# Layer 2 of a four-layer graph network: a node tile's steps add up in PSUM slots that ScalarE copies out, and the node's own product is made in layer 2's node stage

## The reference

```
def _L2_gnn_ref(x, edge_src, edge_dst, adj_vals, w_nbr, w_own, bias):
    h = x @ w_nbr
    msgs = adj_vals[:, None] * h[edge_src]
    agg = jax.ops.segment_sum(msgs, edge_dst, num_segments=x.shape[0])
    return agg + x @ w_own + bias

h = jnp.maximum(_layernorm(x, axis=-1), 0.0)
x = x + _L2_gnn_ref(h, src, dst, edge_weight, L2_gnn_w_nbr, L2_gnn_w_own, L2_gnn_bias)
```

## Time and profile before

| | us |
|---|---|
| median of 3 runs | 6134.13 |
| lowest and highest | 6128.75, 6135.93 |
| span of the profiled execution | 7291.3 |
| edge stage 1 in it | 1650 |
| node stage 2 in it | 129 |
| edge stage 2 in it | 1267 |
| node stage 3 in it | 183 |
| edge stage 3 in it | 1774 |

### The profile page before, as it was taken

One profiled execution on the slowest core, in us unless ns is written; L12 is line 12 of the kernel. 1 busy time (PEld: TensorE's weight loads), 2 busy tenths in 40 slices (PEclk: granted clock), 3 DMA queues, 4 the chain that ended last, 5 costly groups with the idle time before them and its releaser, 6 DMA issues. The chain is left out here.

```text
span 7291.3 us, 78521 instructions
## 1 busy us (share of the span) xinstructions
PE 5030.7 (69%) x19221; PEld 3431.7 (47%) x19221; DVE 4716.5 (65%) x11148; ACT 2046.9 (28%) x5654; POOL 3612.8 (50%) x4189
## 2 busy tenths in 40 slices
PE   3799999999467676667655555557466666666687
PEld 2544444447355555555433333334355455545466
DVE  6699999997355555556644444447366666656776
ACT  3688888886110000000200000001111111111143
POOL 4455555552555555544566666652445454544000
PEclk9899999999666666667777777779576766766798
DMA  5533333333332333222233333332222222222201
GB/s 163 198 98 97 98 98 97 97 96 114 97 81 80 82 82 84 79 76 65 85 92 93 92 92 92 92 118 62 72 77 79 76 79 76 80 72 77 73 24 36
DMA packets 410176, 641.70 MB, mean 88 GB/s; under 512 B 182156, under 2 KB 280032, under 8 KB 409334
## 3 DMA queue, kind: packets, MB, share of 16 engines
q0 software_dynamic: 171200, 474.81, 23.3%
q1 hardware_dynamic: 225664, 149.06, 7.0%
q10 hardware_dynamic: 12896, 13.11, 0.5%
HBM read 563.02 MB, written 69.86 MB: 87 GB/s over the span
## 5 line engine op out<-in xcount | busy, mean ns | idle before, releaser
L250 POOL DMA_INDIRECT G<-table,srcI x1760 | 1667.6, 948 | 1649.2 <-PE pM L502 996.0
L502 PE MATMUL pM<-G,one 128*128 128x260 f32 (+1 forms) x3520 | 1414.9, 509 | 258.6 <-DVE G L373 167.5
L384 DVE TENSOR_TENSOR acc<-acc,pM 128x260 f32 (+1 forms) x1760 | 755.3, 429 | 913.6 <-PE pM L502 570.8
L1357 POOL DMA_INDIRECT G<-table,srcI x880 | 830.5, 944 | 611.7 <-ACT zt L1381 497.5
L572 POOL DMA_INDIRECT G<-table,srcI x880 | 832.9, 947 | 434.4 <-issue 192.8
L608 PE MATMUL pM<-G,one 128*128 128x256 f32 x1760 | 647.4, 508 | 576.2 <-DVE one L581 430.4
L1493 PE MATMUL pM<-zt,one 128*128 128x512 f32 x1760 | 950.2, 621 | 122.1 <-DVE acc L1454 45.4
L502 PEld LDWEIGHTS pM<-G,one 128*128 128x128 f32 x3520 | 757.4, 257 | 437.6 <-DVE G L373 212.6
L1381 ACT ACTIVATE zt<-G,a4S 128x128 f32<-128x128 f32 x2640 | 856.1, 389 | 0.0
L428 ACT ACTIVATE oneT<-pT 128x512 f32<-128x512 f32 x440 | 259.6, 597 | 1966.5 <-PE pT L485 866.8
L608 PEld LDWEIGHTS pM<-G,one 128*128 128x128 f32 x1760 | 382.6, 244 | 836.1 <-DVE one L581 561.1
(11 more groups left out here) (316 smaller groups left out, 6598.2 us busy)
## 6 DMA issues: line engine op xcount, KB each, us to landing
G<-table,srcI POOLq DMA_INDIRECT x3520
a10T<-step_a SPq DMA_DIRECT2D x660, 30.0 KB
far<-step_rec SPq DMA_DIRECT2D x224, 64.0 KB
table<-row SPq DMA_DIRECT2D x100, 128.0 KB
acc<-zero SPq DMA_DIRECT2D x21, 512.0 KB
step_a<-part SPq DMA_DIRECT2D x7, 960.0 KB
table<-row SPq DMA_DIRECT2D x50, 132.0 KB
table<-row SPq DMA_DIRECT2D x50, 130.0 KB
```

The source lines that it names most:

```text
L250: pool.indirect_dma_start(G[:, par * C + j, 0:ROW], None, tab, bass.IndirectOffsetOnAxis(ap=srcI[:, k:k + 1], axis=0)).then_inc(s_g[par * ...
L384: nc.vector.tensor_tensor(to, to, pM[j % R][:, :], ALU.add).then_inc(s_acc, 1)
L502: nc.tensor.matmul(pM[j % R][:, :], one[:, par * C + j, :], G[:, par * C + j, :], start=True, stop=True).then_inc(s_m, 1)
L1357: pool.indirect_dma_start(G[:, k % GS, :], None, table[0], bass.IndirectOffsetOnAxis(ap=srcI[:, k:k + 1], axis=0)).then_inc(s_g[k % GS], 16)
```

## The change

In the edge stage of layer 2, PE no longer writes each step into a tile of its own. PSUM holds 8 slots of one bank each (`pS`); all steps of node tile n add into slot n modulo 8 (`start=False`). At each step three more things happen, at slots read from a list (`node_s`, loaded into `slots`): ACT copies the slot of the node tile before this step's into `sums` (`sums[:, n+1, :]` ends as the sum of tile n; it is copied some 17 times, the last copy is the complete one), DVE clears the slot three tiles ahead by copying zeros (`COMING = 3`), and `mark` goes on, with 8 buffers `one` in place of 4. DVE adds the bias to one tile of x in every 17 steps. The own product moves to node stage 2, as a second product of 256 columns per tile (`pO[1]`), which DVE adds to x in place of the bias; `hT` is gone. In node stage 3 POOL adds `sums` to x (`Layer2End.second`) before the statistics of each tile, and SP saves x to `x3` in five parts, each of ten tiles. Setup makes the three rows of the slot list: four small DVE operations and three small scattered DMAs, and one load (`nodeR`) less.

```diff
-                R = 4
-                one = [se.sb(f"one{j}", [P, P]) for j in range(R)]
-                pM = [se.ps(f"pM{j}", [P, D]) for j in range(R)]
+                RO, EVERY, LATE = 8, K // NT, 3
+                one = [se.sb(f"one{j}", [P, P]) for j in range(RO)]
+                slots = se.sb("slots", [1, 3, KP], I32)
...
-                        def add(k, j):
-                            dve.wait_ge(s_m, k + 1)
-                            freed(dve, s_acc, added(k) - 1)
-                            at = tile(acc, node(k, j))
-                            nc.vector.tensor_tensor(at, at, pM[j % R][:, :], ALU.add).then_inc(s_acc, 1)
...
+                        def mark(k):
+                            freed(dve, s_m, k - RO + 1)
...
+                        def clear(k):
+                            if k % 16 == 0:
+                                at.update(listed(dve, slots[0:1, 2, :], k, SLOTS - 1))
+                            freed(dve, s_out, k - COMING)
+                            dve.wait_ge(s_zero, k + 1)
+                            nc.vector.tensor_copy(sum_of(at[k]), nought[:, :]).then_inc(s_zero, 1)
...
+                    @block.scalar
+                    def _(act):
...
+                            if k % 16 == 0:
+                                at.update(listed(act, slots[0:1, 0, :], k, SLOTS - 1))
+                                to.update(listed(act, nodeA[0:1, :], k, NT - 1))
+                            freed(act, s_m, k)
+                            freed(act, s_out, k)
+                            nc.scalar.activation(tile(sums, to[k]), sum_of(at[k]), ACT.Copy).then_inc(s_out, 1)
...
+                            pe.wait_ge(s_zero, max(1, k - COMING + 2))
+                            pe.wait_ge(s_one, k + 1)
+                            pe.wait_ge(s_g[k % u], k // u * 16 + 16)
+                            nc.tensor.matmul(sum_of(at[k]), one[k % RO][:, :], G[k % u][:, :], start=False, stop=True,
+                                             skip_group_check=True).then_inc(s_m, 1)
...
             def dve_end(dve, n, j, pO, row, aux, s_ae, b):
-                return nc.vector.tensor_tensor(tile(x_sb, n), tile(x_sb, n), b[1][:, :], ALU.add)
+                return nc.vector.tensor_tensor(tile(x_sb, n), tile(x_sb, n), pO[1][:, :], ALU.add)
...
+                def stores(self, sp, n):
+
+                    if n % (NT // 5) == 1:
+                        some = slice(n - 1, n - 1 + NT // 5)
+                        sp.wait_ge(self.s_plus, n - 1 + NT // 5)
+                        sp.dma_start(x3.rearrange("(t p) c -> p t c", p=P)[:, some, :], x_sb[:, some, :]).then_inc(self.s_x3, 16)
...
+                def second(self, pool, n):
+                    pool.tensor_tensor(x_sb[:, n, :], x_sb[:, n, :], self.sums[:, n + 1, :], ALU.add).then_inc(self.s_plus, 1)
```

More of the change, by code:

```diff
@@ L34 @@
 H1, H3 = 4, 8
+SLOTS, COMING = 8, 3
 def build(nc, a, out):
@@ L576, in _ @@
                     def _(dve):
[L577 to L581, removed]
-                                                    ALU.is_equal, ALU.mult).then_inc(s_one, 1)
-                        def add(k, j):
-                            dve.wait_ge(s_m, k + 1)
-                            freed(dve, s_acc, added(k) - 1)
[L587 to L591, removed]
-                                dve.wait_ge(s_acc, added(k))
-                                nc.vector.tensor_tensor(acc[:, n, :], acc[:, n, :], pO[n % 2][:, :], ALU.add).then_inc(s_acc, 1)
@@ L594, in _ @@
-                        steps(dve, u, (AHEAD, load), (0, mark), (LAG, add))
-                    @block.sync
-                    def _(sp):
-                        sp.dma_start(w_sb[:, :, :], w_own.rearrange("(c p) n -> p c n", p=P)).then_inc(s_w, 16)
+                        nc.vector.memset(nought[:, :], 0.0)
+                        nc.vector.memset(pS[:, :, 0:D], 0.0).then_inc(s_zero, 1)
+                        at = {}
+                        dve.wait_ge(s_list, 16)
+                        def mark(k):
+                            freed(dve, s_m, k - RO + 1)
+                            nc.vector.tensor_scalar(one[k % RO][:, :], iota[:, :], relS[:, k:k + 1], wS[:, k:k + 1],
+                                                    ALU.is_equal, ALU.mult).then_inc(s_one, 1)
@@ L600, in _ @@
                     @block.tensor
                     def _(pe):
-                        pe.wait_ge(s_w, 16)
-                        def scatter(k, j):
-                            pe.wait_ge(s_one, k + 1)
-                            gathered(pe, u, s_g, k, j)
-                            freed(pe, s_acc, added(k - R))
-                            nc.tensor.matmul(pM[j % R][:, :], one[j % R][:, :], G[j][:, :], start=True, stop=True).then_inc(s_m, 1)
-                            n = own_at(k)
-                            if n is not None:
-                                freed(pe, s_acc, added(EVERY * (n - 1) - 1) + 1 if n >= 2 else 0)
-                                for c in range(2):
-                                    ins = nc.tensor.matmul(pO[n % 2][:, :], hT[:, n, c * P:(c + 1) * P], w_sb[:, c, :], start=(c == 0), stop=(c == 1))
-                                ins.then_inc(s_o, 1)
@@ L958, in _ @@
                                 sp.dma_start(node_f.rearrange("(b p) -> p b", p=P), nkc[:, :]).then_inc(s_ndd, 16)
+                                for q in range(3):
+                                    sp.dma_start(node_s[q, :].rearrange("(b p) -> p b", p=P), slot[:, q, :]).then_inc(s_ndd, 16)
                             sp.wait_ge(s_w1, 128)
@@ L1037, in _ @@
                             link(nc.vector.tensor_scalar(base[:, :], nk[:, :], float(-P), None, ALU.mult))
+                            for q, ahead in enumerate((SLOTS - 1, 0, COMING)):
+                                link(nc.vector.tensor_scalar(slot[:, q, :], nkc[:, :], float(ahead), None, ALU.add))
+                            link(nc.vector.tensor_scalar(slot[:, :, :], slot[:, :, :], SLOTS - 1, None, ALU.bitwise_and))
                             nc.vector.tensor_copy(nki[:, :], nkc[:, :]).then_inc(s_nd, 1)
```

120 lines of the change are left out of this document (74 added, 46 removed).

## The result

The changed kernel takes 6153.48 us (median of 8 runs, 6148.62 to 6157.1), the kernel before 6133.26 in the same series: ratio 1.0033, 95% interval [1.0023, 1.0043]. It is 20 us slower. The forecast was 6159, its own range 6147 to 6185.

What follows compares the result with a forecast made beforehand. Edge stage 2 was taken to be bound by POOL's gathers, near 1100 us in a timed run. Edge stage 2 0, node stage 2 +18, node stage 3 +5, setup +2: 6134 + 25 = 6159 us, likeliest 6147 to 6185, whole 6060 to 6215.

Steps and rivals of the forecast that it cites:

- Edge stage 2, 0 us: Edge stage 2: added operations stay under POOL's 1.25 us per gather, so no change; bounds -170 and +150 us.
- most of PE's holes belong to the profiled execution: Edge stages 1 to 3: PE's late spells mostly absent from timed runs, leaving at most 234 us over the floor.
- the first rival: Edge stages: PE's holes are real and deeper rings close them, half to all of 170 us; 5990 to 6075, chance 0.22.
- Node stage 2, +18 us: Node stage 2: the second product adds 11 us over 9 rounds and 7 us in the last eight tiles.
- two turns (4.6) still fit into 5.9, three turns take 6.9. So a round goes from 11.3 to 12.6 at most: +1.3, of which I take 1.2: Node stage 2, five-tile rounds: PE at 2.3 us a tile lengthens each round, 11 us over 9 rounds.
- The +7 for the last eight tiles: Node stage 2, last eight tiles without `scales`: their ends go from 1.3 to 2.2 us apart, +7 us.
- The second rival: Node stage 2: the second product is hidden; total 6122 to 6146 us, no change, chance 0.2.
- The other end, +50 at the low clock: Node stage 2: at the low clock the product costs 1.7 us more a tile, the stage +50 us.
- Node stage 3, +5 us: Node stage 3: DVE contends with POOL's additions, 10 rounds x 0.5 us = 5 us, from 0 to 10.
- +0.6: Start of node stage 3: additions, `scales` and a statistics precede DVE's first copy, 12.4 us against 11.8, about +0.6.
- Setup, +2 us: Setup: four DVE operations and 2688 four-byte elements during DVE's 24.4 us wait, +2 us; below 1, above 5.
- Behind the last gather, 0 us: After edge stage 3's last gather to the end: no change forecast, 0 us.

Runs made afterwards that it cites:

- e5: The changed kernel with its slot list made by four DVE operations in edge stage 2, without scattered DMAs, second chip: 7321.87 us against 7306.35, ratio 1.0023.
- e1: The kernel before, unchanged, profiled again on a chip where it takes what the timed runs took: span 6123.1 us.
- e6: The changed kernel with both products in node stage 2, but DVE adding the bias from SBUF instead of the own product from PSUM: 7341.01 us against 7306.35, ratio 1.0056.
- e3: The changed kernel without the own product in node stage 2, DVE adding the bias from SBUF as before: 6152.03 us, ratio to the kernel before 1.0035.
- e8: The changed kernel without POOL's 50 additions in node stage 3 and the waits for them: 7329.82 us against 7306.35, ratio 1.0040.
- e4: The kernel before with the slot list's four DVE operations and three scattered DMAs added to setup, unused: 6146.79 us against 6133.85, ratio 1.0024.
- e9: The changed kernel with its slot list made by DVE in edge stage 2, without scattered DMAs, third chip: 6141.55 us against 6135.25, ratio 1.0012.
- e10: The kernel before with the bias added in edge stage 2 and one scattered list less in setup: 6122.95 us against 6135.25, ratio 0.9983.
- e2: The changed kernel with the slot list's three scattered DMAs moved behind the load of x: 6147.35 us, ratio to the kernel before 1.0026.

## Why the prediction was right, and where it was not

**Edge stage 2, 0 us: right, with one reason wrong.** POOL's gather row is untouched (833.5 and 833.3 us busy, 947 ns each), and the stage stays 1110. The operations added came out as estimated: the copy of zeros 429 ns (taken: 0.42), ACT's copy 383, as in the earlier trace rows, and PE is busy for 955 / 880 = 1.09 us a step at a granted clock of 0.58 (taken: 0.92 to 1.1). One thing had no price: `mark` went from 352 to 431 ns, and DVE is busy for 0.84 us a step, not 0.63; why wasn't tried, and under 1.25 it costs nothing. A stretch of the changed kernel's timeline in this stage:

```profile
3399.51 0.95 POOL L551 DMA_INDIRECT G<-table,srcI  x1 [0.30 <-issue]
...
3400.76 0.95 POOL L551 DMA_INDIRECT G<-table,srcI  x1 [0.30 <-issue]
...
3401.28 0.38 ACT L602 ACTIVATE sums<-pS  x1 [0.81 <-PE pS L616]
...
3401.80 0.43 DVE L577 COPY pS<-nought 128x256 f32 x1 [0.29 <-ACT sums L602]
3402.01 0.95 POOL L551 DMA_INDIRECT G<-table,srcI  x1 [0.30 <-issue]
```

The gathers follow each other at 1.25 us without a wait, and in that time the other engines, which wait for each other in turn, do their step. The prediction's estimate of 0.33 us for a copy with an SBUF source was too low here. It comes from a row of the Trainium skill, "VectorE: DVE Perf Modes", section on the TRN2 errata, and the same section says that this row under-predicts the time of a single operation; the 429 ns agree with that. What was wrong is "most of PE's holes belong to the profiled execution". They go with the chip: the kernel before takes 7284 to 7329 us in all 28 timed runs on the second chip, and the profiles taken there have the holes. The first profile's chip isn't on record, but its 7291 us lie in that range. The conclusion held because the runs that were forecast came from a chip without the holes, which the prediction couldn't know: that part is luck. And the first rival fails where the holes are real too: with eight `one` buffers and slots, e5's edge stage 2 took 1272.4 us on the second chip, against 1266.0 for the kernel before in the first profile.

**Node stage 2, +18 us: wrong, +0.8.** The step that failed is "two turns (4.6) still fit into 5.9, three turns take 6.9. So a round goes from 11.3 to 12.6 at most: +1.3, of which I take 1.2". POOL's row that begins a round, in e1:

```profile
3028.27 0.20 POOL L764 TENSOR_TENSOR mean<-bn 128x5 f32<-128x5 f32 x1 [2.48 <-DVE bn L817]
...
3039.55 0.20 POOL L764 TENSOR_TENSOR mean<-bn 128x5 f32<-128x5 f32 x1 [2.49 <-DVE bn L817]
```

and in the changed kernel, with ACT's copies out of PSUM between:

```profile
3045.79 0.20 POOL L764 TENSOR_TENSOR mean<-bn 128x5 f32<-128x5 f32 x1 [2.06 <-DVE bn L815]
...
3046.02 0.38 ACT L1680 ACTIVATE row<-pO 128x256 f32<-128x256 f32 x1 [1.07 <-PE pO L859]
...
3047.96 0.38 ACT L1680 ACTIVATE row<-pO 128x256 f32<-128x256 f32 x1 [1.08 <-PE pO L859]
...
3050.91 3.65 POOL L1674 TENSOR_TENSOR acc<-acc,xr 128x256 f32<-128x256 f32 x5
...
3056.62 0.20 POOL L764 TENSOR_TENSOR mean<-bn 128x5 f32<-128x5 f32 x1 [2.06 <-DVE bn L815]
```

A round went from 11.28 down to 10.83. Two terms were off. A turn that PE bounds takes 1.94 us (3046.02 to 3047.96), not 2.3: PE runs at the full clock there (granted 1.00 over this round, 0.80 in e1's), and the 1.4 I started from held more than PE's own work, for at the full clock two transposes follow each other in e1 after 1.12 us (3029.84, 3030.96). Five turns of 1.94 are 9.7 us and fit into a round of 11.3: in e6, with both products and the old operand, the round stays at 11.30. (The prediction's own figures, 5.9 + 6.9, would have been 12.8, not 12.6.) And I costed DVE's end at nothing, as an addition for an addition. Its operand moved from SBUF to PSUM, and beside POOL's additions that is 0.41 us in place of 0.94, on the mean of the stage 411 ns in place of 498; the earlier trace rows had shown the effect on L1667, and I used it for node stage 3 only. e3 and e6 split it: the product +5.7 us, the operand -4.8. The +7 for the last eight tiles held nearly: from the end of the last `scales` to the last copy it is 9.2 us in e1 and 15.0 in the changed kernel, +5.8. The second rival ("the second product is hidden") was right for the rounds and for the sum of the stage, but not for its end, and it gave the total wrongly. The other end, +50 at the low clock, didn't come: the stage's granted clock rose to 0.92.

**Node stage 3, +5 us: measured +1.3.** The 5 us were for DVE beside POOL's additions. From PE's first product to the end of the stage it takes 170.8 us in e1 and 172.9 in the changed kernel, and 170.4 in e8 against 173.6 in e5: 2.1 and 3.2 us, so the mechanism is there and the size was high. The start, which I had put at "+0.6", came out as a gain of 0.9 us: the additions cost 3.3 there (e8), and without the one save of x beside the weights' loads the start gains more than that.

**Setup, +2 us: wrong, and the size that mattered.** "2688 four-byte elements that go out while DVE waits 24.4 us for gathered rows; below 1, above 5". The wait was read as cover. It is a wait for DMAs, and more DMAs lengthen it. Windows of four microseconds of the setup, e1 and then the changed kernel, each with its DMA queues from 44 to 48 us (q0 has the gathers):

```profile
44.00:48.00 4.00, 0.00 (x0) 0.00 (x0) 0.00 (x0) 0.00 (x0) 2.92 (x4) 1.00 1.10 73
48.00:52.00 4.00, 0.00 (x0) 0.00 (x0) 1.01 (x2) 0.00 (x0) 3.09 (x4) 1.00 0.62 143
...
q1 hardware_dynamic: 335, 0.21, 79.4%
q0 software_dynamic: 38, 0.09, 31.0%
```

```profile
44.00:48.00 4.00, 0.00 (x0) 0.00 (x0) 0.00 (x0) 0.00 (x0) 2.98 (x4) 1.00 1.93 1
48.00:52.00 4.00, 0.00 (x0) 0.00 (x0) 0.00 (x0) 0.00 (x0) 2.89 (x4) 1.00 1.48 21
...
DMA packets 1196, 0.00 MB, mean 1 GB/s; under 512 B 1196, under 2 KB 1196, under 8 KB 1196
q1 hardware_dynamic: 1196, 0.00, 193.4%
```

In the changed kernel the DMA engines move 1 GB/s from 44 to 48 us, in 1196 small packets (the share adds up the packets' times, which overlap, and so goes to 1.93), and no packet of the gathers' queue begins in that time: the gathers of the destinations stand still beside the elements. The Trainium skill, "DMA: Bandwidth & Descriptors", says in the table of its section "Specifications" that a transfer below 512 bytes is a read-modify-write, and in the table of "Rules for kernel authors" that a last dimension that isn't contiguous becomes one descriptor per element. By that these 10.5 KB are 2688 small writes; the trace agrees with 2800 more packets under 512 B on the page. That each is a read-modify-write no run here shows. The slot list's DMAs with their DVE operations cost 12.9 us (e4), and with the DMAs gone 14 of the 20 us go (from 1.0033 to 1.0012): by the medians the term is 13 to 14 us, by the profiles 18.7.

**Behind the last gather, 0 us: +3.9, not foreseen.** The code is the same in both. Two parts can be told apart. One goes with the program: from the issue of the last store to the end it takes 10.0 to 10.1 us in all seven profiles with the old edge stage 2 and 11.5 to 11.7 in all seven with the new one, whatever the chip. The other is a pattern in the two batch norms. ACT's squares (a ring of four with DVE's and PE's parts) wait for DVE 9 times in the changed kernel and 10 in e9, 4 times in e1 and e10, and from its first to its last square each norm takes some 1.2 us longer (23.7 and 23.3 us against 22.3 and 22.2); 1.0 of that comes back between the two. This pattern doesn't follow the program: e2, with the new edge stage 2, has the short norms (4 waits, 512.8 us behind the last gather), and the first profile, with the old one, the long ones (8 waits, 23.6 and 23.3 us). Why the same instructions fall into another pattern, and what the 1.6 us are, wasn't tried.

So the total was right by luck, by two errors of opposite sign: 17 us too much in node stage 2, and in the setup 17 too little by the profiles, 11 to 12 by the medians.

## What to carry over

A wait for DMAs covers work on engines, not further DMAs: before small transfers are put into such a wait, ask which transfers share the DMA engines with them, and count their elements, for bytes didn't set the price here. An operation that is exchanged for one of the same shape isn't free of price when its operand moves between SBUF and PSUM and another engine works beside it; and where POOL and DVE set a stage's round, a second product per tile costs nothing in the rounds and shows only in the tiles behind them (5.7 us here), while one DVE addition per tile less gives 13 us, of which 5 went back where the addition was put (e10). A rewritten inner loop gains nothing while the gathers ahead of it keep their 1.25 us.

## What the runs showed of the hardware that was not expected

The same kernel takes 6134 us on two of the chips and 7306 and 7444 on two others, steadily. The difference lies in three stages: by the profiles of the kernel before, edge stage 1 takes 1650 against 1167 us, edge stage 2 1266 against 1110, and edge stage 3 to the end 2212 against 1702, while the setup (133, 131), edge stage 0 (1438, 1423) and node stages 2 and 3 (129.7 and 128.9, 183.9 and 183.7) agree within 2%. In the first profile's edge stage 2 PE stands still for 3.46 and for 6.94 us before two rows, and DVE around them:

```profile
4200.84 0.42 DVE L588 TENSOR_TENSOR acc<-acc,pM 128x256 f32 x1 [3.48 <-DMA xr<-x]
4201.58 0.70 PE L608 MATMUL pM<-G,one 128*128 128x256 f32 x2 [3.46 <-DVE one L581]
4205.06 0.42 DVE L588 TENSOR_TENSOR acc<-acc,pM 128x256 f32 x1 [3.53 <-DMA xr<-x]
4208.48 0.42 DVE L593 TENSOR_TENSOR acc<-acc,pO 128x256 f32<-128x256 f32 x1 [3.00 <-DMA xr<-x]
4208.82 0.34 DVE L581 TENSOR_SCALAR one<-iota,relS,wS 128x128 f32<-128x128 f32 x1
4209.21 4.41 PE L608 MATMUL pM<-G,one 128*128 128x256 f32 x12 [6.94 <-DVE one L581]
```

PE's second wait ends right behind the mark of 4208.82, but that mark stands behind DVE's additions, and the addition of 4205.06, which needs a matmul, starts 2.8 us after PE's last one ended by its row (4202.28). (The DMA that the rows name was done long before.) So the engines wait for each other, and the profile has no row for what is late. The windows of the two gaps, the same profile:

```profile
4198.20:4201.50 3.30, 0.00 (x0) 0.00 (x0) 0.66 (x2) 0.00 (x0) 2.53 (x3) 1.00 0.35 93
4202.30:4209.20 6.90, 0.00 (x0) 0.00 (x0) 1.14 (x4) 0.00 (x0) 2.64 (x3) 0.50 0.27 76
```

One gap lies at the upper of the clock's two levels, 2.4 GHz, and the other at the lower, 1.2 GHz. So the lower level isn't needed for such gaps, and it doesn't make them either: on the quicker chip the same stage has a granted clock of 0.71 on the mean, in the changed kernel 0.58, and there PE has no gap of more than 1.9 us, where it has 119 of over 2 us in the first profile. DMA packets take the same time on both (median 159 ns for the gathers'). What holds the engines up on the slower chips stays open. For a forecast it means that a profile whose span is far from the timed runs may come from another chip, and that holes in it are to be checked against the sum of the stages.
